# Cross-attention of layer 0: values taken with the weights as the stationary operand, denominators by an extra column, and a transpose after the division

## The chip, the cores and the metric

One core of a Trainium2 chip runs the whole program in one launch. The metric is the device time in microseconds (us); the median of three runs of the kernel before is 985.59 us (984.96 to 985.84).

## The reference

A stack of four layers works on x of 8 batches x 256 tokens x 128 features, in float32. Each layer is a cross-attention to a context of 8 x 64 tokens and then a feed-forward part; every part adds its output to x. The change touches only the first part, the attention of layer 0:

```
q  = layernorm(x) @ Wq                 # 16 heads of 8 features
k, v = context @ Wkv                   # one head of 8 features, shared by all 16
sim = (q * 8**-0.5) . k                # 16 heads x 64 keys for each token
attn = softmax(sim - max(sim))
x  = x + (attn . v, heads side by side) @ Wo
```

What has to be computed for one token and one head is a sum over 64 keys of weight times value (8 numbers) and the sum of the 64 weights, by which the 8 numbers are divided.

## The kernel before, in words

The program is written by hand for each engine: TensorE (`pe`), VectorE (`dve`), ScalarE (`act`), GpSimd (`pool`) and the DMA queue (`sp`) each have one list of instructions that runs in order, and semaphores tie them together. The tokens are 16 tiles of 128. The attention of layer 0 is a software pipeline over `for t in range(NT + 3)`, written once in each engine's block; in turn t tile t gets its similarities and older tiles their later steps. For tile u the steps are these.

- **Similarities** (`similarities`, TensorE, called S below): two products with 64 rows each, 512 columns each, into two PSUM banks. VectorE takes the maximum over the keys (L1343) and subtracts it into `simS` (L1346). ScalarE takes the exponential into `simE` (L874).
- **Weights transposed** (`weights_T`, T below): eight 128x128 transposes with `ident` (L1820) put keys on partitions. One chunk of 128 partitions holds the 64 keys of two heads. ScalarE copies the 1024 columns to `simET` (`weight_rows`, recorded at L813).
- **Values** (`values`, V below): 16 products. The stationary operand is a strip of 32 columns of `vstrip` (the values) or of `ostrip` (ones), the moving operand is a chunk of `simET` with 128 columns. Each product writes 32 partitions of bank 6. Four such products for four different groups of 32 partitions follow each other. What comes out is already transposed: features on partitions, tokens in columns, and beside it the denominators, repeated for each feature. VectorE takes the reciprocal of the 128x128 denominators (L1354) and multiplies (L1355) into `y0T`.
- **Output** (`outputs0`, O below): `y0T` times `wo0`, then VectorE adds it to X (L1359).

The order on TensorE in an ordinary turn t is S(t), T(t-1), V(t-2), O(t-3). In the turns 2, 6 and 10, called grouped, four transposes and the projection for the queries of the next four tiles stand among these (`token_rows`, `queries`), and T is cut in two halves. VectorE has, in turn t, the maximum and subtraction of tile t, the reciprocal and product of tile t-2 and the addition of tile t-3; in turn 5 also the statistics of the slot embeddings (`slot_stats`, L1309 to L1318), and after every fourth addition the statistics of the next layer norm (`ln_stats`). After turn 15 the slot transposes (L1884), the next layer norm's transposes (L1789) and the first logits of layer 0's feed-forward part (`logits_slots`) come in between the last steps, and the feed-forward part waits for the last addition to X.

All float32 products are recorded as two instruction pairs (LDWEIGHTS and MATMUL) each; transposes as one pair.

Of the kernel before, what the change touches and what calls it, by code (L numbers as in the profile page):

```python
# [5 lines left out]
ALU = mybir.AluOpType  # L6
# [40 lines left out]
def build_program(nc, A, out):  # L47
    with ExitStack() as ctx:
        def sb(name, shape, dt=F32):
            return ctx.enter_context(nc.sbuf_tensor(name, shape, dt))  # L50

        def sem(name):
            return ctx.enter_context(nc.semaphore(name))
# [50 lines left out]
        wk3 = sb("wk3", [P, D])  # L104
        wv3 = sb("wv3", [P, D])
        wo3 = sb("wo3", [P, D])


        xw = sb("xw", [P, 2 * T + 8 * P], F32R)
# [45 lines left out]
        simE = carve(2, H0 * C)  # L155
        simET = carve(2, H0 * C)
        krep = carve(B * C)
        vstrip = carve(B, 2, P // 4)
        ostrip = carve(2, P // 4)
        y0T = carve(2, P)  # L160
        mx0 = carve(2, H0)
        rden0 = carve(P)
        ctxTd = carve(B * 2 * C)
        slot_raw = carve(ES // P, D)
        slot_n = carve(ES // P, D)
# [155 lines left out]
        se_T = sem("se_T")  # L321
        kv_mm = sem("kv_mm")
        krep_done = sem("krep_done")
        vstrip_done = sem("vstrip_done")
        kbd_done = [sem("kbd_first"), sem("kbd_rest")]
        q_mm = sem("q_mm")
        q_sb = sem("q_sb")
# [4 lines left out]
        et_sb = sem("et_sb")  # L332
        av_ready = sem("av_ready")
        y_ready = sem("y_ready")
        out_ready = sem("out_ready")
        bl_ready = sem("bl_ready")
        bmax_done = sem("bmax_done")
# [237 lines left out]
        def _(pool):  # L575
# [14 lines left out]
                               pattern=[[-1, P]], channel_multiplier=1).then_inc(consts, 1)  # L590
            pool.wait_ge(consts, 1)

            then(pool.memset(headmask[:, :], 1.0))
            then(pool.affine_select(out=headmask[:, :], in_=headmask[:, :], compare_op=ALU.is_ge, fill=0.0, base=0,
                                    pattern=[[-HD, H0]], channel_multiplier=1))
            then(pool.affine_select(out=headmask[:, :], in_=headmask[:, :], compare_op=ALU.is_ge, fill=0.0, base=HD - 1,
                                    pattern=[[HD, H0]], channel_multiplier=-1))
            then(pool.tensor_tensor(rowmask[:, :], headmask[:, 0:H0 // 2], headmask[:, H0 // 2:H0], ALU.add))
            pool.memset(vstrip, 0.0)
            then(pool.memset(ostrip, 0.0))  # L600
            for par in range(2):
                for r in range(2):
                    at = 16 * par + HD * r
                    last = pool.memset(ostrip[C * r:C * r + C, par, at:at + HD], 1.0)
            last.then_inc(consts, 1)
            pool.wait_ge(consts, 2)
            pool.tensor_copy(identb[:, :], ident[:, :])

            def ln_power(L, g):
                s = slice(4 * g, 4 * g + 4)  # L610
# [200 lines left out]
        def _(act):  # L811
            def copy(dst, src):
                return act.activation(dst, src, ACT.Copy)  # L813
# [27 lines left out]
            def queries(g):  # L841
                act.wait_ge(q_mm, g + 1)
                act.activation(qT[:, 512 * g:512 * g + 512], bank(4), ACT.Copy, scale=float(HD) ** -0.5).then_inc(q_sb, 1)

            def weight_rows(u):
                act.wait_ge(et_ready, u + 1)
                if u >= 2:
                    act.wait_ge(av_ready, u - 1)
                copy(simET[:, u % 2, :], psum[:, 4:6, :].rearrange("p a n -> p (a n)")).then_inc(et_sb, 1)
# [4 lines left out]
            for t in range(NT + 3):  # L854
                g = (t + 2) // 4
                if t == 1:
                    act.wait_ge(kv_mm, 2)
                    act.wait_ge(consts, 2)
                    vps = psum[:, 6, 256:256 + B * HD].rearrange("p (b d) -> p b d", b=B)
                    for par in range(2):  # L860
                        for r in range(2):
                            at = 16 * par + HD * r
                            last = copy(vstrip[C * r:C * r + C, :, par, at:at + HD], vps[C * r:C * r + C])
                    last.then_inc(vstrip_done, 1)
                if t % 4 == 2 and t < NT - 2:
                    token_rows(g)
                    queries(g)
                if 1 <= t <= NT:
                    weight_rows(t - 1)
                if t < NT:  # L870
                    act.wait_ge(sim_used, t + 1)
                    if t >= 2:
                        act.wait_ge(et_ready, t - 1)
                    act.activation(simE[:, t % 2, :], simS[:, t % 2].rearrange("p h k -> p (h k)"), ACT.Exp).then_inc(exp_done, 1)  # L874
                if t == NT:

                    act.wait_ge(se_n, 2)
                    for g in range(2):
                        act.wait_ge(se_tp, g + 1)
                        act.activation(seT[:, 512 * g:512 * g + 512], bank(g), ACT.Identity, scale=slot_gs[:, 0:1], bias=slot_gs[:, 1:2])\  # L880
                            .then_inc(se_T, 1)
                    for g in range(2):
                        ln_evac_group(1, g)
# [329 lines left out]
        def _(dve):  # L1213
# [125 lines left out]
            for t in range(NT + 3):  # L1339
# [11 lines left out]
                if 2 <= t <= NT + 1:  # L1351
                    u = t - 2
                    dve.wait_ge(av_ready, u + 1)
                    then(dve.reciprocal(rden0, psum[:, 6, P:2 * P]))  # L1354
                    dve.tensor_tensor(y0T[:, u % 2, :], psum[:, 6, 0:P], rden0, ALU.mult).then_inc(y_ready, 1)  # L1355
                if t >= 3:
                    u = t - 3
                    dve.wait_ge(out_ready, u + 1)
# [402 lines left out]
        def _(pe):  # L1761
# [61 lines left out]
            def values(u):  # L1823
                b = u // TB
                pe.wait_ge(et_sb, u + 1)
                if u == 0:
                    pe.wait_ge(vstrip_done, 1)
                if u >= 1:
                    pe.wait_ge(y_ready, u)
                for k, w in enumerate((vstrip[:, b], ostrip)):  # L1830
                    for par in range(2):
                        for j in range(4):
                            own, at = slice(32 * j, 32 * j + 32), P * (2 * j + par)
                            last = mm(psum[own, 6, P * k:P * k + P], w[:, par, :], simET[:, u % 2, at:at + P], par == 0, par == 1)
                last.then_inc(av_ready, 1)

            def outputs0(u):
                if u == 0:
                    pe.wait_ge(w_slots, 16 * N_SLOTS)
                pe.wait_ge(y_ready, u + 1)  # L1840
                if u >= 1:
                    pe.wait_ge(x_done, u)
                mm(psum[:, 7, 0:D], y0T[:, u % 2, :], wo0[:, :]).then_inc(out_ready, 1)

            def logits_slots(k):
# [20 lines left out]
            for t in range(NT + 3):  # L1866
# [11 lines left out]
                if t == NT:  # L1878

                    pe.wait_ge(se_n, 2)  # L1880
                    pe.wait_ge(sim_used, NT - 1)
                    for g in range(2):
                        for j in range(4):
                            last = pe.transpose(psum[:, g, P * j:P * j + P], slot_n[:, 4 * g + j, :], ident[:, :])  # L1884
                        last.then_inc(se_tp, 1)
                if grouped:
                    values(t - 2)
                    queries(g)
# [12 lines left out]
                if grouped:  # L1901
                    if t >= 3:
                        outputs0(t - 3)
                    pe.wait_ge(q_sb, g + 1)
                    weights_T(t - 1, (0,)).then_inc(et_ready, 1)
                else:
                    if 2 <= t <= NT + 1:
                        values(t - 2)
                    if t >= 3:
                        outputs0(t - 3)  # L1910
# [595 lines left out]
```

## Time and profile before

| | |
|---|---|
| median of three runs | 985.59 us |
| the profiled execution's own time | 984.96 us |
| its span | 983.2 us |
| TensorE busy, whole span | 913.7 us (93%) |
| VectorE busy | 719.9 us (73%) |
| ScalarE busy | 521.5 us (53%) |
| mean granted TensorE clock | 0.967 |

The span is from the first to the last instruction in the trace; the execution's own time lies 1.8 us above it. A busy TensorE in the table is not TensorE at its peak: the ends of matmuls are modelled and contain a latency of some 0.2 us, so the time between the starts of neighbouring instructions says more than their length. "Granted clock" is 1.00 at 2.4 GHz and 0.50 at 1.2 GHz. The attention of layer 0 takes roughly the first 90 us of the span; everything behind it is the same code before and after.

### The profile page before, as it was taken

How to read it: one execution, taken by the hardware profiler on the slowest of the kernel's cores; microseconds unless marked ns; L12 is line 12 of the kernel's file. 1: busy time of each engine (PE TensorE's matmuls, PEld its weight loads, DVE VectorE, ACT ScalarE, POOL GpSimd, SP SyncE). 2: the span in 40 equal slices, each digit the busy share in tenths (PEclk: the TensorE clock that was granted, in tenths of full speed). 3: DMA queues.
4: the chain of work that ended last, by engine and by line, in shares of the span. 5: the costliest groups of instructions: out<-in, count | busy, mean ns of one | idle time of the engine just before them, and what ended most of it. 6: DMA issues, size and time to landing. Idle time of an engine off the chain costs nothing. (4 is left out here: it accounts for less than half of the span.)

```text
span 983.2 us, 16388 instructions
## 1 busy us (share of the span) xinstructions
PE 913.7 (93%) x4925; PEld 700.8 (71%) x4925; DVE 719.9 (73%) x1657; ACT 521.5 (53%) x991; POOL 572.7 (58%) x542
## 2 busy tenths in 40 slices
PE   7897998989896899999999999999999889999796
PEld 5555775666694856888888888888887766667564
DVE  6897776899464788766666666666667888886865
ACT  3455665544634256666666666666663334453354
POOL 5512544677513156777777777777776538884500
PEclk9999999999997989999999999999999689999998
DMA  6000000322000000000000000000002000000001
GB/s 193 1 2 2 1 1 11 88 71 66 12 1 27 2 9 14 25 25 24 24 24 24 24 24 24 24 24 24 25 3 108 1 0 1 1 1 1 1 11 33
DMA packets 27113, 24.01 MB, mean 24 GB/s; under 512 B 3420, under 2 KB 23988, under 8 KB 26804
## 3 DMA queue, kind: packets, MB, share of 16 engines
q1 hardware_dynamic: 27059, 23.34, 8.0%
q8 instruction: 29, 0.48, 0.2%
q14 instruction: 25, 0.20, 0.1%
HBM read 22.28 MB, written 1.05 MB: 24 GB/s over the span
## 5 line engine op out<-in xcount | busy, mean ns | idle before, releaser
L1763 PE MATMUL psum<-xw 128*128 128x512 f32 x1248 | 324.3, 396 | 3.9 <-DVE xw L1400 2.6
L664 POOL TENSOR_TENSOR hh<-arena,hh 128x512 fp32r<-128x512 f32 x176 | 228.2, 1296 | 81.7 <-ACT hh L813 80.0
L1763 PEld LDWEIGHTS psum<-xw 128*128 128x128 f32 x1248 | 233.4, 189 | 56.5 <-issue 7.2
L1599 DVE TENSOR_TENSOR psum<-psum,arena 128x512 f32<-128x512 f32 x176 | 123.1, 700 | 99.6 <-PE psum L1763 93.2
L813 ACT ACTIVATE hh<-arena 128x512 fp32r<-128x512 f32 x228 | 143.1, 629 | 47.7 <-DVE arena L1698 45.3
L1046 ACT ACTIVATE arena<-psum 128x512 f32<-128x512 f32 x176 | 105.3, 598 | 119.0 <-PE psum L1763 118.9
L1763 PE MATMUL psum<-hh,wdn 128*128 128x512 f32 x528 | 148.4, 390 | 0.2 <-POOL hh L664 0.2
L1604 DVE TENSOR_TENSOR arena<-psum,arena 128x512 f32<-128x512 f32 x176 | 121.7, 692 | 8.9 <-DVE psum L1599 2.9
L1763 PEld LDWEIGHTS psum<-hh,wdn 128*128 128x128 f32 x528 | 98.9, 188 | 21.1 <-POOL hh L664 0.5
L1763 PE MATMUL psum<-arena 128*32 128x128 f32 (+7 forms) x1032 | 94.0, 307 | 12.8 <-ACT arena L813 6.5
L612 POOL TENSOR_TENSOR rstd<-veps,neghalf 128x4 f32<-128x4 f32 x28 | 28.2, 1010 | 106.1 <-DVE veps L1238 76.0
L1763 PEld LDWEIGHTS psum<-arena 128*32 128x32 f32 (+4 forms) x1032 | 69.1, 148 | 25.0 <-issue 11.4
L813 ACT ACTIVATE arena<-psum 128x512 f32<-128x512 f32 (+7 forms) x84 | 57.1, 694 | 50.4 <-PE psum L1763 19.6
L701 POOL TENSOR_TENSOR hh<-arena,hh 128x512 fp32r<-128x512 f32 x48 | 62.1, 1295 | 33.3 <-ACT hh L813 31.8
L764 POOL TENSOR_TENSOR tail<-tail 128x512 f32<-128x512 f32 x32 | 33.3, 1041 | 43.4 <-DVE tail L1370 43.4
L1763 PE MATMUL psum<-hh,w2r 128*128 128x512 f32 x144 | 46.7, 417 | 2.0 <-POOL hh L701 1.0
L624 POOL TENSOR_TENSOR xw<-egu,xw 128x256 fp32r<-128x256 f32 x32 | 27.6, 864 | 31.8 <-ACT xw L813 31.5
L891 ACT ACTIVATE tail<-arena,tail 128x256 f32<-128x256 f32 x64 | 32.0, 500 | 26.1 <-DVE tail L1333 26.1
L928 ACT ACTIVATE tail<-psum,ebias 128x512 f32<-128x512 f32 x32 | 22.0, 688 | 44.5 <-PE psum L1763 36.9
L635 POOL TENSOR_TENSOR arena<-arena,xn (+1 forms) x32 | 42.8, 1343 | 1.2 <-ACT xn L813 1.2
L1690 DVE SCALAR_TENSOR_TENSOR arena<-psum,arena 128x512 f32<-128x512 f32 x48 | 33.1, 691 | 11.7 <-PE psum L1763 9.6
L1763 PE MATMUL psum<-xw,w2r 128*128 128x512 f32 x144 | 41.6, 401 | 0.0
(288 smaller groups left out, 1536.1 us busy)
## 6 DMA issues: line engine op xcount, KB each, us to landing
egu<-in_w SPq DMA_DIRECT2D x44, 128.0 KB, 2.0
egu<-in_egu SPq DMA_DIRECT2D x16, 256.0 KB, 2.6
edn<-in_w SPq DMA_DIRECT2D x44, 64.0 KB, 1.8
edn<-in_edn SPq DMA_DIRECT2D x16, 128.0 KB, 2.0
arena<-in_w SPq DMA_DIRECT2D x1, 1536.0 KB, 6.8
X<-in_x SPq DMA_DIRECT2D x4, 256.0 KB, 4.6
arena<-in_conv SPq DMA_DIRECT2D x1, 1024.0 KB, 8.8
out<-X SPq DMA_DIRECT2D x4, 256.0 KB, 2.3
```

The source lines that it names most:

```text
L612: pool.tensor_tensor(rstd[:, s], veps[:, s], neghalf[:, s], ALU.pow).then_inc(ln_rstd, 1)
L635: pool.tensor_tensor(part, part, wide(shift_row(b).unsqueeze(1), 2, N), ALU.subtract).then_inc(pt_shifted, 1)
L664: pool.tensor_tensor(hh[:, s % 4, 1, :], h1[:, s % 2, :], hh[:, s % 4, 0, :].bitcast(F32), ALU.subtract).then_inc(hh_lo, 1)
L701: pool.tensor_tensor(hh[:, n % 4, 1, :], h2[:, n % 2, :], hh[:, n % 4, 0, :].bitcast(F32), ALU.subtract).then_inc(hh_lo, 1)
L764: pool.tensor_tensor(qb[:, k % 4], qb[:, k % 4], wide(recB[:, k % 4].unsqueeze(2), 2, N), ALU.mult)\
L813: return act.activation(dst, src, ACT.Copy)
L891: last = act.activation(qb[:, k % 4, c, :], logit_part(k // 4, 2 * (k % 4) + c, 1).rearrange("p a n -> p (a n)"), ACT.Exp, scale=-1.0, bia ...
L1046: act.activation(sil[:, k, :], bank(k), ACT.Silu).then_inc(nl_done, 1)
L1599: dve.tensor_tensor(bank(2 + k), bank(2 + k), sil[:, k, :], ALU.mult).then_inc(prod_done, 1)
L1604: dve.tensor_tensor(h1[:, k, :], bank(2 + k), rwb[:, s // 4, own], ALU.mult).then_inc(hid_done, 1)
L1690: dve.scalar_tensor_tensor(v2w[:, n % 3, :], bank(q), 0.0, cB[:, 0 if n < 4 * NG else 1, 512 * q:512 * q + 512], ALU.max, ALU.mult)\
L1763: return pe.matmul(dst, lhsT=lhsT, rhs=rhs, start=start, stop=stop)
```

## The change

The roles of the operands in V are exchanged. The transposed weights of two heads (a 128x128 chunk of `simET`) are now stationary, eight of them, and the moving operand is `vaug`, 18 columns: for each of the two heads 8 value columns and one column of ones. What comes out has tokens on partitions and, per head, 8 sums and one denominator. VectorE's reciprocal has 16 elements per partition in place of 128, and its product of 128x128 reads the denominators broadcast over the 8 features. Since O needs features on partitions, a new step follows: TensorE transposes `y0` (`outputs_T0`, called T0 below) and ScalarE copies the result to `y0T` (`output_rows`). In turn t, T0(t-3) stands behind T(t-1) and ahead of V(t-2), in grouped turns behind `token_rows`; `output_rows(t-3)` stands behind `weight_rows(t-1)` and ahead of the exponential, in grouped turns ahead of `queries`. GpSimd's constants at the start change (`vaug` in place of `vstrip` and `ostrip`, and an array `ltmask` that nothing reads).

```diff
+        ltmask = sb("ltmask", [P, 8, 8])
...
-        vstrip = carve(B, 2, P // 4)
-        ostrip = carve(2, P // 4)
+        vaug = carve(B, 2, HD + 1)
+        y0 = carve(2, H0, HD)
         y0T = carve(2, P)
         mx0 = carve(2, H0)
-        rden0 = carve(P)
+        rden0 = carve(2, H0)
...
@@ GpSimd, constants
-            pool.memset(vstrip, 0.0)
-            then(pool.memset(ostrip, 0.0))
-            for par in range(2):
-                for r in range(2):
-                    at = 16 * par + HD * r
-                    last = pool.memset(ostrip[C * r:C * r + C, par, at:at + HD], 1.0)
-            last.then_inc(consts, 1)
-            pool.wait_ge(consts, 2)
-            pool.tensor_copy(identb[:, :], ident[:, :])
+            then(pool.affine_select(out=ltmask[:, :, :], in_=ltmask[:, :, :], compare_op=ALU.is_ge, fill=0.0, base=-1,
+                                    pattern=[[1, 8], [-1, 8]], channel_multiplier=0))
+            then(pool.memset(vaug, 0.0))
+            pool.memset(vaug[0:C, :, 0, HD:HD + 1], 1.0)
+            then(pool.memset(vaug[C:P, :, 1, HD:HD + 1], 1.0))
+            pool.tensor_copy(identb[:, :], ident[:, :]).then_inc(consts, 1)
...
@@ ScalarE
+            def output_rows(u):
+                act.wait_ge(yT_ready, u + 1)
+                if u >= 2:
+                    act.wait_ge(out_ready, u - 1)
+                copy(y0T[:, u % 2, :], psum[:, 7, 256:384]).then_inc(yT_sb, 1)
...
-                    for par in range(2):
-                        for r in range(2):
-                            at = 16 * par + HD * r
-                            last = copy(vstrip[C * r:C * r + C, :, par, at:at + HD], vps[C * r:C * r + C])
-                    last.then_inc(vstrip_done, 1)
+                    copy(vaug[0:C, :, 0, 0:HD], vps[0:C])
+                    copy(vaug[C:P, :, 1, 0:HD], vps[C:P]).then_inc(vaug_done, 1)
                 if t % 4 == 2 and t < NT - 2:
                     token_rows(g)
+                if t % 4 == 2 and t < NT - 2:
+                    if t >= 3:
+                        output_rows(t - 3)
                     queries(g)
-                if 1 <= t <= NT:
                     weight_rows(t - 1)
+                else:
+                    if 1 <= t <= NT:
+                        weight_rows(t - 1)
+                    if t >= 3:
+                        output_rows(t - 3)
...
@@ VectorE
-                    then(dve.reciprocal(rden0, psum[:, 6, P:2 * P]))
-                    dve.tensor_tensor(y0T[:, u % 2, :], psum[:, 6, 0:P], rden0, ALU.mult).then_inc(y_ready, 1)
+                    av = psum[:, 6, 0:H0 * (HD + 1)].rearrange("p (h k) -> p h k", k=HD + 1)
+                    then(dve.reciprocal(rden0[:, u % 2, :], av[:, :, HD]))
+                    if u >= 2:
+                        dve.wait_ge(yT_ready, u - 1)
+                    dve.tensor_tensor(y0[:, u % 2], av[:, :, 0:HD], wide(rden0[:, u % 2, :].unsqueeze(2), H0, HD), ALU.mult)\
+                        .then_inc(y_ready, 1)
...
@@ TensorE
-                for k, w in enumerate((vstrip[:, b], ostrip)):
-                    for par in range(2):
-                        for j in range(4):
-                            own, at = slice(32 * j, 32 * j + 32), P * (2 * j + par)
-                            last = mm(psum[own, 6, P * k:P * k + P], w[:, par, :], simET[:, u % 2, at:at + P], par == 0, par == 1)
+                for j in range(H0 // 2):
+                    w = 2 * (HD + 1)
+                    last = mm(psum[:, 6, w * j:w * j + w], simET[:, u % 2, P * j:P * j + P],
+                              vaug[:, b].rearrange("p h k -> p (h k)"))
                 last.then_inc(av_ready, 1)
+
+            def outputs_T0(u):
+                pe.wait_ge(y_ready, u + 1)
+                if u >= 1:
+                    pe.wait_ge(x_done, u)
+                pe.transpose(psum[:, 7, 256:384], y0[:, u % 2].rearrange("p h k -> p (h k)"), ident[:, :]).then_inc(yT_ready, 1)
 
             def outputs0(u):
                 if u == 0:
                     pe.wait_ge(w_slots, 16 * N_SLOTS)
-                pe.wait_ge(y_ready, u + 1)
-                if u >= 1:
-                    pe.wait_ge(x_done, u)
+                pe.wait_ge(yT_sb, u + 1)
...
+                if grouped and t >= 3:
+                    outputs_T0(t - 3)
                 if grouped:
                     values(t - 2)
                     queries(g)
...
                 else:
+                    if t >= 3:
+                        outputs_T0(t - 3)
                     if 2 <= t <= NT + 1:
                         values(t - 2)
```

## Rows read from the trace of the kernel before

**Rows 1.** Stretches: length, busy (x instructions) per engine, granted clock, DMA share, GB/s.
```profile
60.00:70.00 10.00, 8.97 (x105) 5.89 (x105) 9.65 (x21) 5.78 (x7) 3.09 (x3) 1.00 0.01 2
```

**Rows 2.** Timeline, one ordinary turn: start us, length us, engine, line, operation.
```profile
69.65 0.30 PEld L1763 LDWEIGHTS psum<-arena 64*128 64x128 f32 x4
...
70.94 0.86 PEld L1820 LDWEIGHTS psum<-ident,arena 128*128 128x128 f32 x8 [0.99 <-ACT arena L874]
...
71.10 1.22 DVE L1343 TENSOR_REDUCE arena<-psum 128x16 f32<-128x1024 f32 x1
71.97 0.81 PEld L1763 LDWEIGHTS psum<-arena 128*32 128x32 f32 x32 [0.17 <-issue]
...
72.36 1.23 DVE L1346 TENSOR_TENSOR arena<-psum,arena 128x1024 f32<-128x1024 f32 x1
72.98 0.30 PEld L1763 LDWEIGHTS psum<-wo,arena 128*128 128x128 f32 x2 [0.20 <-issue]
...
73.39 0.30 PEld L1763 LDWEIGHTS psum<-arena 64*128 64x128 f32 x4
...
73.61 1.06 ACT L874 ACTIVATE arena<-arena 128x1024 f32<-128x1024 f32 x1 [0.51 <-DVE arena L1346]
```

**Rows 3.** Timeline at the end of the stage: 128*128 work behind 128*128 work.
```profile
88.40 0.30 PEld L1763 LDWEIGHTS psum<-wo,arena 128*128 128x128 f32 x2 [0.20 <-issue]
...
88.62 0.73 PEld L1763 LDWEIGHTS psum<-xnT,seT 128*128 128x128 f32 x4
```

**Rows 4.** Projection of the values (starts: first to last us), then a whole-span group.
```profile
L1763 PE MATMUL psum<-wv,arena x16: 256/256/277, 13.4 to 15.1; 128*128 128x8 f32 x16
...
L1763 PE MATMUL psum<-arena 128*128 128x129 f32 x256 | 28.8, 275 | 0.3 <-issue 0.3
```

**Rows 5.** Groups of the whole span: reciprocals of two sizes.
```profile
L1354 DVE RECIPROCAL arena<-psum 128x128 f32<-128x128 f32 x16 | 15.2, 951 | 4.4 <-PE psum L1763 4.3
...
L1370 DVE RECIPROCAL tail<-tail 128x2 f32<-128x2 f32 x32 | 5.1, 160 | 0.4 <-ACT tail L891 0.4
```

**Rows 6.** Timeline, ScalarE's copies from PSUM, of 64 and of 512 columns.
```profile
16.14 0.89 ACT L813 ACTIVATE arena<-psum 64x64 f32<-64x64 f32 x4
...
20.46 0.60 ACT L813 ACTIVATE xnT<-psum 128x512 f32<-128x512 f32 x1 [0.45 <-PE psum L1800]
```

**Rows 7.** Timeline, similarities: the first behind the first grouped turn, and the last.
```profile
23.94 0.30 PEld L1763 LDWEIGHTS psum<-arena 64*128 64x128 f32 x4 [0.17 <-issue]
...
77.17 0.30 PEld L1763 LDWEIGHTS psum<-arena 64*128 64x128 f32 x4
```

**Rows 8.** Timeline, the grouped turn 10 and the T after it.
```profile
56.50 0.30 PEld L1763 LDWEIGHTS psum<-arena 64*128 64x128 f32 x4
...
57.56 0.42 PEld L1800 LDWEIGHTS psum<-ident,xn 128*128 128x128 f32 x4 [0.76 <-issue]
...
61.56 0.30 PEld L1763 LDWEIGHTS psum<-arena 64*128 64x128 f32 x4 [0.17 <-issue]
...
63.69 0.86 PEld L1820 LDWEIGHTS psum<-ident,arena 128*128 128x128 f32 x8 [1.83 <-ACT arena L874]
```

**Rows 9.** Timeline, slot statistics on VectorE and the V that follows.
```profile
35.87 1.64 DVE L1312 BATCH_NORM_STATS2 arena<-arena 128x6 f32<-128x128 f32 x8
...
39.85 1.08 PE L1763 MATMUL psum<-arena 128*32 128x128 f32 x32 [2.37 <-DVE arena L1355]
```

**Rows 10.** Timeline, the last tile: T and the last addition.
```profile
83.79 0.86 PEld L1820 LDWEIGHTS psum<-ident,arena 128*128 128x128 f32 x8 [2.14 <-ACT arena L874]
...
90.65 0.29 DVE L1359 TENSOR_TENSOR X<-X,psum 128x128 f32<-128x128 f32 x1
```

**Rows 11.** Stretches around two falls of the clock, columns as in rows 1.
```profile
14.00:17.30 3.30, 2.36 (x21) 2.11 (x20) 3.23 (x11) 1.82 (x5) 1.50 (x2) 1.00 1.03 338
17.30:20.70 3.40, 3.40 (x17) 1.55 (x20) 2.83 (x4) 2.32 (x3) 3.24 (x4) 0.51 0.71 202
41.20:44.60 3.40, 3.40 (x12) 2.17 (x10) 2.90 (x6) 0.60 (x1) 2.79 (x2) 0.51 0.00 0
```

More of the change, by code:

```diff
@@ L323, in build_program @@
         krep_done = sem("krep_done")
-        vstrip_done = sem("vstrip_done")
+        vaug_done = sem("vaug_done")
         kbd_done = [sem("kbd_first"), sem("kbd_rest")]
@@ L334, in build_program @@
         y_ready = sem("y_ready")
+        yT_ready = sem("yT_ready")
+        yT_sb = sem("yT_sb")
         out_ready = sem("out_ready")
@@ L591, in _ @@
             pool.wait_ge(consts, 1)
-            then(pool.memset(headmask[:, :], 1.0))
+            pool.memset(headmask[:, :], 1.0)
+            then(pool.memset(ltmask[:, :, :], 1.0))
             then(pool.affine_select(out=headmask[:, :], in_=headmask[:, :], compare_op=ALU.is_ge, fill=0.0, base=0,
@@ L1826, in values @@
                 if u == 0:
-                    pe.wait_ge(vstrip_done, 1)
+                    pe.wait_ge(vaug_done, 1)
                 if u >= 1:
                     pe.wait_ge(y_ready, u)
-                for k, w in enumerate((vstrip[:, b], ostrip)):
-                    for par in range(2):
-                        for j in range(4):
-                            own, at = slice(32 * j, 32 * j + 32), P * (2 * j + par)
-                            last = mm(psum[own, 6, P * k:P * k + P], w[:, par, :], simET[:, u % 2, at:at + P], par == 0, par == 1)
-                last.then_inc(av_ready, 1)
+                for j in range(H0 // 2):
+                    w = 2 * (HD + 1)
+                    last = mm(psum[:, 6, w * j:w * j + w], simET[:, u % 2, P * j:P * j + P],
+                              vaug[:, b].rearrange("p h k -> p (h k)"))
+                last.then_inc(av_ready, 1)
+            def outputs_T0(u):
[3 more added lines that the diff above has]
+                pe.transpose(psum[:, 7, 256:384], y0[:, u % 2].rearrange("p h k -> p (h k)"), ident[:, :]).then_inc(yT_ready, 1)
             def outputs0(u):
```

## The prediction

> **What bounds the kernel now.** I read the stretches of ten microseconds first, because the change lies in the first 90 us alone. Between 60 and 70 us VectorE is busy for 9.65 of 10 us and TensorE for 8.97 [rows 1]: VectorE is full, TensorE nearly. Then the timeline of one ordinary turn, read by starts [rows 2]. S(13) starts at 69.65 and S(14) at 73.39: 3.74 us for a turn. On VectorE the maximum starts at 71.10, the subtraction at 72.36 (1.26) and runs 1.23, and the reciprocal of 0.95 [rows 5], product and addition fill the rest of the turn. On TensorE the pieces of a turn are, from start to start: T to V 1.03 (70.94 to 71.97), V to O 1.01, O to the next S 0.41. S itself takes 1.06 where the next step needn't wait (56.50 to 57.56) [rows 8]; here T starts 1.29 after S, since it waits for the exponential (0.99 us of idle weight loader). So TensorE alone could do a turn in 1.06 + 1.03 + 1.01 + 0.41 = 3.51 us, only 0.23 below the present one. VectorE sets the turn and TensorE stands close behind: whatever is taken from the one and given to the other counts almost in full.
>
> **Gaps on TensorE.** In rows 2 the eight loads of T take 0.86 us, but V starts 1.03 after them; the 32 loads of V take 0.81, but O starts 1.01 after; O's two loads (0.11 apart) are done after 0.22, S starts after 0.41. At each of these places 0.17 to 0.20 us pass, and at each the shape of the array's tile changes (64\*128, 128\*128, 128\*32). Where one 128\*128 step follows another there is no gap although semaphores are waited on too: O starts at 88.40 and the logits behind it at 88.62, 0.22 for two loads [rows 3]. The Trainium skill has a rule for this, "TensorEngine Tiling (Array Packing)", section Key Properties: changing the tiling mode drains TensorE, changing only the tile does not. Rows 2 and 3 agree with it. I take it that gaps stand at changes of shape; the other reading, a gap at every hand-over with a wait, is a rival below.
>
> **The change, part by part.**
>
> *V on TensorE.* Before: 32 instruction pairs with 32 weight columns, 0.81 us and a gap on either side, 0.17 + 0.81 + 0.20 = 1.18. After: 8 products are 16 pairs with 128 weight columns and 18 moving ones. The nearest row is the projection of the values, 128x8 with 128\*128 weights: 16 starts in 13.4 to 15.1, 0.113 apart, at clock 1.00 [rows 11]. With 129 moving columns the group of 256 takes 28.8 us, also 0.1125 each [rows 4]. So from 8 to 129 moving columns the price is the same, it is the weights that are paid, and 18 columns lie between: 16 x 0.1125 = 1.80 us. Bounds: not under the 0.107 of T's loads (1.71), and not over the sum with both gaps (2.17).
>
> *T0 on TensorE.* One more pair, 0.11 us as in T (0.86 / 8). It stands between T and V, all 128\*128, so the gaps before and behind V go. Sum: V and T0 take 1.80 + 0.11 = 1.91 where 1.18 stood, +0.73 per turn. The ordinary turn on TensorE becomes 3.51 + 0.74 = **4.25 us**.
>
> The Trainium skill would price V lower: "TensorE: Matmul & The Clock Gate", section Back-to-back issue gap, gives about 81 ns per matmul for streams of weight load and matmul with 128 columns. By that V would be an estimated 16 x 0.081 = 1.30. Rows 4, at 0.1125, don't bear it out, and the sum goes by them.
>
> *VectorE.* The reciprocal falls from 951 ns for 128 elements to somewhere between 160 (2 elements) and 951; along the line through both rows, 6.3 ns per element, 16 elements take 0.25 us [rows 5]. The product stays 128x128. VectorE's turn becomes 3.74 - 0.70, about 3.05 us: covered by TensorE's 4.25. The gain of 0.70 is real and buys nothing beyond the 0.23 that TensorE leaves.
>
> *ScalarE.* Copying 128 columns from PSUM lies between 0.22 (0.89 / 4 for 64) and 0.60 (512) [rows 6]; by the line 0.28. It waits behind `weight_rows`, which starts when T is done and takes about 1.0: T0's result is in SBUF some 1.1 + 1.05 + 0.28 = 2.45 us after T's start, O wants it after 0.86 + 0.11 + 1.80 = 2.77. Hidden, with 0.3 us to spare; at 0.60 it is just hidden. What is queued behind it is the exponential. A tile's way from S through maximum, subtraction and exponential to its own T takes at least 1.15 for S, 1.26, 1.25 and 1.06 [rows 2] and some 0.1 between, 4.8 us; the new TensorE comes to that T 4.25 + 1.06 = 5.3 after S. Also hidden, closely.
>
> *Start-up.* GpSimd's constants and the fewer copies at turn 1 lie beside work that waits for DMA and VectorE: 0.
>
> **The sum.** From S(3) at 23.94 to S(15) at 77.17 are 53.23 us [rows 7]. After the change these twelve turns are:
> - seven ordinary ones, 4.25 each: 29.75.
> - three behind a grouped turn (3, 7, 11). There T waits for the exponential, which ScalarE does late: S at 61.56, T at 63.69, 2.13 [rows 8]. This stays. 2.13 + 0.86 + 0.11 + 1.80 + 0.41 = 5.31 each: 15.93.
> - grouped turn 10: 61.56 - 56.50 = 5.06 [rows 8], plus 0.74: 5.80.
> - grouped turn 6, where VectorE is late by the slot statistics. Before, V(4) stood until 39.85, 2.37 us idle, [rows 9] and the clock then fell [rows 11]. The statistics start at 35.87; with reciprocal 0.95, product and addition ahead of V's release at 39.85 they last some 2.56. Counted from S(5): subtraction at 2.44, statistics from 3.6 to 6.15, short reciprocal, product and addition until 6.95, T0(3) at 6.97, V, then 2.40 until S(7) as in turn 10: 11.28. S(6) is at 4.25, so turn 6 takes 7.03.
>
> Together 58.5: **+5.3**. Ahead of S(3): V(0) is on the path, partly at the low clock: +0.7. Behind S(15): T(15) stood 6.62 us after it, because VectorE was late with its maximum; TensorE stood idle for 2.14 [rows 10]. VectorE now has time in every turn: I put the end of the statistics after addition 11 at 1.6 us after S(15), and 1.26 + 1.25 + 1.06 + 0.05 later T comes, at 5.2: -1.4. From T(15) to the last addition were 6.86 us (90.65 - 83.79) [rows 10]. After: T 0.86, T0 0.11, V(14) 1.80, O 0.22, norm transposes 0.86, T0 0.11, V(15) 1.80, O 0.22, logits 0.86, then T0(15), copy, O and addition 0.9: 7.75, +0.9. Sum of all: 0.7 + 5.3 - 1.4 + 0.9 = +5.5.
>
> *The clock.* At 17.3 it falls to 0.51 (1.2 GHz) for 3.4 us, after a stretch at 1.00 with the narrow 128x8 products, an idle time and a T; it falls again at 41.2 [rows 11], after the idle time before V(4) [rows 9]. The new V is work of just that narrow kind. In ordinary turns S and T stand close on either side of it and I expect full clock; in the three turns with the 1 us wait for T, and in turn 6, a fall is possible. One costs at most half its 3.4 us, 1.7. The fall at 41.2 is already out of turn 6's new figure. I add **1.0** for one of these at less than its bound.
>
> 984.96 (the execution's own time, span 983.2 plus 1.8) + 6.5 = 991.5. The median lies 0.6 above this execution: **992 us**.
>
> **Rivals.**
> 1. *Gaps at every hand-over.* If what costs 0.17 to 0.20 is the wait and not the shape, T to T0, T0 to V and V to O keep one each: 0.54 per turn over 14 turns, +7.5: 999.5. For it: each of the gaps in rows 2 has waits as well. Against it: rows 3.
> 2. *The clock stays low often.* If the narrow V brings it down in four or five turns, +1.5 each on top: 998 to 1000. For it: rows 11. Against it: T and S in the same turn.
> 3. *The weights load as fast as before's, or nearly.* The strips of V before are loaded 0.81 / 32 = 0.025 apart for 32 columns [rows 2], T's 128 columns 0.107; if the new V lay halfway, at 0.066 a pair, it would take 1.06. TensorE's ordinary turn would be 3.51, and VectorE's 3.05 under it; fifteen turns give back 0.74 each, 11 us, and the relief of VectorE in turn 6 and at T(15) is left over: 991.5 - 11 = 980.5, **faster than before. It decides from 0.085 us per pair down** (15 x 16 x 0.027 = 6.5, the whole forecast loss). For it: the moving columns are few, so nothing but the load is left to pay. Against it: two groups in rows 4 at 0.1125 with 8 and with 129 columns. By the Trainium skill's 81 ns of above (TensorE: Matmul & The Clock Gate, Back-to-back issue gap) the time would be an estimated 991.5 - 7.5 = 984, on the edge of this rival.
> 4. *TensorE's surplus is absorbed.* Turn 6 and the end lose more stall than I counted (idle 2.37 and 2.14 us before), and no clock falls: 986 to 988.
>
> **How the numbers follow.** Forecast 0.62 (988 to 995), rival 1 0.10, rival 2 0.09, rival 3 0.08, rival 4 0.11. The range 986 to 998 leaves out most of rival 3 and the top of 1 and 2. A measurement of this kernel tells about 0.2%, 2 us, from no change. Slower than 987.6: forecast, rivals 1 and 2 and a little of 4: 0.83. Within: most of rival 4, part of 3: 0.11. Faster: the rest of 3: 0.06.
>
> **What the changed profile would show.** V: 16 pairs 128\*128 with 128x18, starts 0.11 apart, T0 one pair, no gap between T, T0, V and O, one of 0.2 before S. Ordinary turns 4.25 us from S to S, TensorE with no idle time in them, VectorE at about seven tenths in 60 to 70 us. Reciprocal near 0.25 us. The last addition of the stage near 96 us. Everything behind it as before but for shifted falls of the clock. I am wrong if the pairs of V lie clearly under 0.1 us apart, if O waits for ScalarE, or if the turns in which the granted clock is 0.50 are many.

## The result, and the profile after

The changed kernel takes 993.88 us in the median (991.86 to 996.98), the kernel before beside it 985.72: ratio 1.0078, 95% interval 1.0048 to 1.0107. By these medians, of four executions each, it is slower by 8.2 us; 992 was forecast, 986 to 998 was the range. All 25 executions of the changed kernel on record for this result lie between 990.05 and 999.47 us, with a median of 992.99. The profiled execution is the longest of them, 999.47 us with a span of 997.7; another execution of the same kernel, taken later, took 990.75 us with a span of 989.0. The two are read side by side. The last addition of this stage starts at 103.27 us in the one and at 95.72 in the other, so 7.55 of the 8.7 us between the spans lie in this stage, and there the granted clock is what differs; 1.15 lie behind it, in code that is the same.

First the ordinary turn, in the timeline of the changed kernel (start, length, engine, line, operation; L1836 is T, L1856 is T0, the 128x128 loads at L1779 are V, and the 64x128 loads S). It answers to [rows 2] (times in us; LDWEIGHTS is the load of a stationary operand):

```profile
55.29 0.30 PEld L1779 LDWEIGHTS psum<-arena 64*128 64x128 f32 x4
...
55.82 0.60 PE L1779 MATMUL psum<-arena 64*128 64x512 f32 x2
56.35 0.85 PEld L1836 LDWEIGHTS psum<-ident,arena 128*128 128x128 f32 x8 [0.76 <-ACT arena L886]
...
57.17 0.14 PEld L1856 LDWEIGHTS psum<-ident,arena 128*128 128x128 f32 x1
...
57.28 1.87 PEld L1779 LDWEIGHTS psum<-arena 128*128 128x128 f32 x16
...
57.48 1.19 ACT L815 ACTIVATE arena<-psum 128x1024 f32<-128x1024 f32 x2 [1.64 <-PE psum L1836]
...
58.98 1.06 ACT L886 ACTIVATE arena<-arena 128x1024 f32<-128x1024 f32 x1 [0.31 <-DVE arena L1358]
59.07 0.30 PEld L1779 LDWEIGHTS psum<-wo,arena 128*128 128x128 f32 x2
...
59.28 0.26 DVE L1367 RECIPROCAL arena<-psum 128x16 f32<-128x16 f32 x1 [0.34 <-PE psum L1779]
59.49 0.30 PEld L1779 LDWEIGHTS psum<-arena 64*128 64x128 f32 x4
```

T to V takes 0.93 (56.35 to 57.28) with T0 in it, V to O 1.79, O to S 0.42: V's 16 loads stand 0.112 apart, and there is no gap between T, T0, V and O, only the one ahead of S. VectorE's reciprocal is down from 951 ns to about 0.25 us and now waits for TensorE; ScalarE's copy of 128 columns lies inside the 1.19 at 57.48 (two copies merged) and ends 0.4 us before O. TensorE holds the turn: 4.20 us from S (55.29) to S (59.49).

Now the clock. The stretches of the profiled execution, then of the later one (columns as in [rows 1]):

```profile
20.00:40.00 20.00, 17.83 (x125) 13.21 (x124) 15.35 (x47) 10.20 (x14) 8.94 (x10) 1.00 0.01 1
40.00:60.00 20.00, 18.84 (x124) 14.70 (x126) 14.10 (x30) 9.43 (x13) 7.86 (x6) 0.91 0.00 1
60.00:80.00 20.00, 18.97 (x101) 14.27 (x99) 11.17 (x25) 7.64 (x12) 3.09 (x3) 0.75 0.01 1
80.00:95.00 15.00, 14.70 (x101) 11.69 (x97) 10.79 (x24) 6.51 (x9) 3.09 (x3) 0.88 0.01 2
...
69.80:83.50 13.70, 13.70 (x54) 10.24 (x54) 6.45 (x10) 3.43 (x5) 0.00 (x0) 0.50 0.00 0
```

```profile
20.00:40.00 20.00, 18.03 (x125) 13.40 (x125) 14.71 (x45) 10.17 (x14) 8.75 (x10) 1.00 0.00 1
40.00:60.00 20.00, 18.56 (x131) 14.24 (x132) 14.76 (x32) 9.47 (x13) 8.06 (x6) 1.00 0.00 1
60.00:80.00 20.00, 18.97 (x138) 14.62 (x136) 14.71 (x30) 9.98 (x15) 3.09 (x3) 1.00 0.01 2
80.00:95.00 15.00, 14.35 (x117) 12.81 (x115) 8.32 (x26) 8.76 (x14) 3.09 (x3) 1.00 0.00 1
```

Look at the granted clock, the third figure from the end of a line. The later execution has 1.00 throughout. The profiled one has a whole 13.7 us at 0.50, 1.2 GHz, from 69.8 on. What TensorE did just before was this (profiled execution): a grouped turn, S(11), one microsecond without work until the exponential was there, T, T0 and the narrow V, in the middle of which the clock fell. The later execution has the same wait and the same V in turn 11 and no fall, so these do not bring one about each time.

```profile
65.24 0.30 PEld L1779 LDWEIGHTS psum<-arena 64*128 64x128 f32 x4 [0.17 <-issue]
...
67.37 1.09 PE L1836 MATMUL psum<-ident,arena 128*128 128x128 f32 x8 [1.00 <-ACT arena L886]
...
68.30 2.10 PEld L1779 LDWEIGHTS psum<-arena 128*128 128x128 f32 x16
...
71.05 0.51 PEld L1779 LDWEIGHTS psum<-arena 64*128 64x128 f32 x4 [0.23 <-issue]
...
74.82 3.54 PEld L1779 LDWEIGHTS psum<-arena 128*128 128x128 f32 x16
...
79.01 0.51 PEld L1779 LDWEIGHTS psum<-arena 64*128 64x128 f32 x4 [0.23 <-issue]
```

At the low clock V takes 3.54 and the turn 7.96 (71.05 to 79.01) in place of 4.20. Turns 11, 12 and 13 together cost 6.4 us more than their like elsewhere. The 0.91 between 40 and 60 us is a shorter fall, 3.4 us from 42.6 on, in turn 6, behind the wait ahead of T0(3).

### The profile page after: what moved, and what is told of

Read it like the earlier page. It is cut to its first block and busy times, and to the rows that moved or that the text cites. A ratio compares the mean times of both kernels' runs of the same rounds, so it can differ in the third digit from the quotient of the medians.

```text
span 997.7 us, 15949 instructions
## 1 busy us (share of the span) xinstructions
PE 930.0 (93%) x4685; PEld 722.5 (72%) x4685; DVE 709.9 (71%) x1657; ACT 522.4 (52%) x1005; POOL 572.8 (57%) x541
## 5 line engine op out<-in xcount | busy, mean ns | idle before, releaser
L1779 PE MATMUL psum<-xw 128*128 128x512 f32 x1248 | 322.7, 394 | 3.9 <-DVE xw L1416 2.6
L1779 PEld LDWEIGHTS psum<-xw 128*128 128x128 f32 x1248 | 232.3, 188 | 56.0 <-issue 7.2
L1779 PE MATMUL psum<-hh,wdn 128*128 128x512 f32 x528 | 148.4, 390 | 0.2 <-POOL hh L666 0.2
L1779 PE MATMUL psum<-arena 128*128 128x18 f32 (+7 forms) x776 | 111.5, 322 | 10.3 <-ACT arena L815 6.5
L1779 PEld LDWEIGHTS psum<-hh,wdn 128*128 128x128 f32 x528 | 98.9, 188 | 21.1 <-POOL hh L666 0.5
L1779 PEld LDWEIGHTS psum<-arena 128*128 128x128 f32 (+3 forms) x776 | 90.1, 196 | 19.9 <-ACT arena L815 9.3
L815 ACT ACTIVATE arena<-psum 128x512 f32<-128x512 f32 (+8 forms) x98 | 59.7, 634 | 64.6 <-PE psum L1836 31.2
L1779 PE MATMUL psum<-hh,w2r 128*128 128x512 f32 x144 | 46.7, 416 | 2.2 <-POOL hh L703 0.8
L1779 PE MATMUL psum<-xw,w2r 128*128 128x512 f32 x144 | 41.7, 402 | 0.0
```

The source lines that it names most:

```text
L1779: return pe.matmul(dst, lhsT=lhsT, rhs=rhs, start=start, stop=stop)
```

## The experiments

**Half the loads.** V with 4 products of 36 columns:

```diff
-                for j in range(H0 // 2):
-                    w = 2 * (HD + 1)
-                    last = mm(psum[:, 6, w * j:w * j + w], simET[:, u % 2, P * j:P * j + P],
-                              vaug[:, b].rearrange("p h k -> p (h k)"))
+                for j in range(H0 // 4):
+                    w = 4 * (HD + 1)
+                    pair = b // 2 * 2
+                    last = mm(psum[:, 6, w * j:w * j + w], simET[:, u % 2, P * j:P * j + P],
+                              vaug[:, pair:pair + 2].rearrange("p b h k -> p (b h k)"))
```

> The changed kernel, but V has 4 products of 36 moving columns in place of 8 of 18: the same columns go through, half the weights are loaded (the chunks of heads 8 to 15 are left out, so these heads' sums are not computed). Theory (V costs what its 16 weight loads cost, 0.112 us each): V takes 0.90 in place of 1.79, TensorE alone could do a turn in 3.3, the way from S through the exponential (4.8 us) then holds the turn at about 3.55; thirteen turns give back 0.65, some 8 to 9 us, and falls of the clock become rare: about 981 to 983, faster than the kernel before. Rival (V's price is a fixed latency or the moving columns): V stays near 1.8 and the time near 990 to 994.

Measured: 985.05 us (981.67 to 986.53), ratio to before 0.9987 (0.9975 to 0.9999). One ordinary turn of it:

```profile
65.28 0.30 PEld L1779 LDWEIGHTS psum<-arena 64*128 64x128 f32 x4
...
66.34 0.86 PEld L1836 LDWEIGHTS psum<-ident,arena 128*128 128x128 f32 x8 [0.76 <-ACT arena L886]
...
67.27 0.97 PEld L1779 LDWEIGHTS psum<-arena 128*128 128x128 f32 x8
...
68.71 0.30 PEld L1779 LDWEIGHTS psum<-wo,arena 128*128 128x128 f32 x2 [0.47 <-ACT arena L815]
...
69.13 0.30 PEld L1779 LDWEIGHTS psum<-arena 64*128 64x128 f32 x4
```

Half the loads with the same moving columns in all are 0.97 where 1.87 stood: V pays per pair, whether 18 or 36 columns move. This kernel halves the number of pairs together with the weight columns, so it doesn't separate the two; that the columns count is read from V before, whose pairs with 32 weight columns start 0.025 apart [rows 2]. But the turn is 3.85, not 3.55, and O now waits 0.47 for ScalarE: the copy to `y0T` stands behind 1024 columns of weights. The step that was "hidden, with 0.3 us to spare" binds as soon as V shrinks. The time expected, 981 to 983, was missed by 2 to 4 us; 0.3 us in each of twelve turns is of that size.

**One pair per product (fp32r).** `simET` is laid into `hh` and `vaug` into `wdn`, both fp32r tensors idle in this stage:

```diff
-        simET = carve(2, H0 * C)
+        simET = hh[:, 0:2].rearrange("p a b n -> p a (b n)")
...
-        vaug = carve(B, 2, HD + 1)
+        vaug = wdn[:, 0].rearrange("p h n -> p (h n)")[:, 0:B * 2 * (HD + 1)].rearrange("p (b h k) -> p b h k", b=B, h=2)
...
```

GpSimd's constants for `vaug` are written through a float32 view of it; that is all else that differs.

> The changed kernel with simET and vaug in the rounded 32-bit type (fp32r), so that each of V's 8 products is one pair in place of two. Theory (a pair costs its weight load, 0.11): V takes 0.90 in place of 1.79, as in the run with half the loads, but with all heads computed; turn about 3.55, time 981 to 983. Rival (an fp32r load of 128 columns costs more than half of the two float32 loads): V between 0.9 and 1.8, time between 983 and 991.

Measured: 985.07 us (981.53 to 987.07), ratio 0.9987 (0.9972 to 1.0003). V is 8 pairs in 0.97 us, so an fp32r load costs what a float32 load costs and there are half as many; the turn is 3.85 with the same wait of 0.47 for ScalarE. The time, expected at 981 to 983, was missed for the same reason.

**VectorE's gain alone.** In the kernel before:

```diff
-                    then(dve.reciprocal(rden0, psum[:, 6, P:2 * P]))
-                    dve.tensor_tensor(y0T[:, u % 2, :], psum[:, 6, 0:P], rden0, ALU.mult).then_inc(y_ready, 1)
+                    then(dve.reciprocal(rden0[:, 0:H0], psum[:, 6, P:P + H0]))
+                    dve.tensor_tensor(y0T[:, u % 2, :].rearrange("p (h k) -> p h k", k=HD), psum[:, 6, 0:P].rearrange("p (h k) -> p h k", k=HD),
+                                      wide(rden0[:, 0:H0].unsqueeze(2), H0, HD), ALU.mult).then_inc(y_ready, 1)
```

> The kernel before, but VectorE's reciprocal reads 16 columns in place of 128 and the product reads them broadcast (the division is then by the wrong denominators; V and O are as before). This is the change's gain on VectorE alone. Theory (TensorE stands 0.23 us behind VectorE, and the way through the exponential at 3.6): ordinary turns of 3.74 and 3.78 fall to 3.5 to 3.6, each of twelve gives 0.1 to 0.2, turn 6 and the wait for T(15) shrink by 0.7 to 1.4 each: 3 to 4 us, 982 to 983. Rival (VectorE's 0.70 counts in full): 0.7 in each of 15 turns, 975.

Measured: 982.48 us (980.45 to 982.97), ratio 0.9961 (0.9950 to 0.9973), in the size that was expected: 3.6 us, not the 10 that 0.70 in each turn would be. But it does not come from where it was expected. S starts in its trace at

```profile
64.20 0.30 PEld L1764 LDWEIGHTS psum<-arena 64*128 64x128 f32 x4
...
67.71 0.30 PEld L1764 LDWEIGHTS psum<-arena 64*128 64x128 f32 x4
...
71.45 0.30 PEld L1764 LDWEIGHTS psum<-arena 64*128 64x128 f32 x4
```

3.51 and 3.74 apart, where the kernel before had 3.51 and 3.74 in the same places: these turns are not VectorE's. Of the twelve turns from S(3) on only one ordinary turn (3.78 to 3.52) and turn 6 (8.89 to 6.52) shrank, and the wait for T(15). The 0.1 to 0.2 expected in each turn did not come, and turn 6 gave 2.4 in place of 0.7 to 1.4; in this trace it has no fall of the clock, in that of the kernel before it has one [rows 11]. That the sum came out as expected is luck.

**Without the new step.** T0 and the copy left out, O reads `y0`:

```diff
-                pe.wait_ge(yT_sb, u + 1)
-                mm(psum[:, 7, 0:D], y0T[:, u % 2, :], wo0[:, :]).then_inc(out_ready, 1)
+                pe.wait_ge(y_ready, u + 1)
+                if u >= 1:
+                    pe.wait_ge(x_done, u)
+                mm(psum[:, 7, 0:D], y0[:, u % 2].rearrange("p h k -> p (h k)"), wo0[:, :]).then_inc(out_ready, 1)
...
```

> The changed kernel without T0 and without ScalarE's copy: O takes y0 as it is (which leaves the transposition out of the result; all else is done). Theory (in the changed kernel TensorE holds the turn and the copy is hidden behind V): T0 costs its one weight load, turns fall from 4.20 to 4.10, 5.27 to 5.17, 5.75 to 5.65. Rival (O in fact waits for the copy now and then): more than 0.2 per turn.

Measured, in one execution: turns of 4.09 (53.83 to 57.92), 5.16 and 5.64, so T0 costs 0.11 a turn and the copy nothing; 989.28 us, with one fall of the clock, in turn 6.

```profile
53.83 0.30 PEld L1775 LDWEIGHTS psum<-arena 64*128 64x128 f32 x4
...
57.92 0.30 PEld L1775 LDWEIGHTS psum<-arena 64*128 64x128 f32 x4
```

**Gap by shape or by wait.** A product is added at the head of V, behind its waits, with 32 weight columns in one kernel (first line) and with 128 in the other (second line):

```diff
+                mm(psum[0:32, 6, 160:168], ident[:, 0:32], ident[:, 0:8])
...
+                mm(psum[:, 6, 160:168], ident[:, :], ident[:, 0:8])
```

> The changed kernel with one tiny product added between T0 and V: 32 weight columns, 8 moving ones (128*32), into unused columns of V's bank. Two loads of 32 columns are 0.05 us. Theory (gaps stand where the tile's shape changes): its turns grow by 0.05 and two gaps of 0.17 to 0.20, from 4.20 to 4.6. Rival (gaps stand where there are waits): it adds no wait, turns grow by 0.05 to 4.25.

> As the run before, but the added product is full (128*128, 8 moving columns): two loads of 128 columns, 0.22 us of work. Theory of the shape: no gap, turns from 4.20 to 4.42, so the larger product costs less than the smaller. Rival of the waits: the same 4.42, but then the smaller one at 4.25.

Measured, in one execution each: ordinary turns of 4.56 with the small product, 4.42 with the large one. The product with a quarter of the weights costs 0.36, the full one 0.22. (The times, 998.40 and 993.83 us, hold falls of the clock at different places, the small one's 10.2 us long from 17.6 on, and are not compared.) First the small, then the large one in their timelines; the first view ends ahead of V's last two loads:

```profile
73.02 0.14 PEld L1857 LDWEIGHTS psum<-ident,arena 128*128 128x128 f32 x1
...
73.33 0.14 PEld L1779 LDWEIGHTS psum<-ident 128*32 128x32 f32 x2 [0.17 <-issue]
...
73.48 1.64 PEld L1779 LDWEIGHTS psum<-arena 128*128 128x128 f32 x14
```

```profile
70.97 0.14 PEld L1857 LDWEIGHTS psum<-ident,arena 128*128 128x128 f32 x1
...
71.08 0.30 PEld L1779 LDWEIGHTS psum<-ident 128*128 128x128 f32 x2
...
71.31 1.87 PEld L1779 LDWEIGHTS psum<-arena 128*128 128x128 f32 x16
```

T0 to the small product is 0.31 for a single load, to the large one 0.11. The gap belongs to the change of shape, as [rows 3] had it: both products stand behind the same waits, and only the small one has gaps. The Trainium skill's rule (TensorEngine Tiling (Array Packing), Key Properties), that changing the tiling mode drains TensorE, agrees with it.

**The clock.** Products of `ident` fill TensorE's waits, ahead of T in turns 3, 7 and 11 and ahead of T0(3) in turn 6:

```diff
+            def fill(k, n):
+                for _ in range(n):
+                    mm(psum[:, k, 384:512], ident[:, :], ident[:, :])
...
+                if t == 6:
+                    fill(5, 5)
...
+                    if t in (3, 7, 11):
+                        pe.wait_ge(et_sb, u)
+                        fill(4, 4)
                     pe.wait_ge(exp_done, u + 1)
```

> The changed kernel, with products of ident by ident put where TensorE waits: four ahead of T in turns 3, 7 and 11 (0.86 us of work in a wait of 1.0) and five ahead of T0(3) in turn 6. Nothing is left out. Theory (the runs of the changed kernel differ by 990 to 999.5 because the clock falls in this stage in some): granted clock 1.00 from 20 to 95 us, turn 6 about 7.1, all turns at 4.20, 5.27, 5.75; time 989 to 991 with runs within 1 us of each other. Rival (the spread comes from later stages, or the narrow V itself brings the clock down): spread stays several us, median 992 to 995; or, if the fillers come too late for the wait, each adds up to 0.9 us.

Measured: 990.46 us (989.64 to 992.68), ratio to before 1.0056 (1.0037 to 1.0075). All turns are as if undisturbed: 4.20, 5.27, 5.75 and 7.12 for turn 6. The five executions lie within 3.0 us, not within the 1 expected. Then the changed kernel again, and each kind of filler alone:

> The changed kernel itself, on the same chip and beside the same runs of before as the next two. Theory (its runs differ by where the clock falls in this stage): median 992 to 995 with runs over 6 us apart, while the kernel before stays within 3. Rival (the spread was that of the other chip): within 3 us as before.

> The changed kernel with only the five products of ident ahead of T0(3) in turn 6; nothing in turns 3, 7 and 11. Theory (turn 6 holds the fall at 42 us, 1.4 us, and the three waits of 1 us for T each hold a rarer, costlier one): turn 6 at 7.1, one of the other falls still in some runs: median 991 to 993, spread 3 to 6 us. Rival (turn 6 alone is the cause): as with all fillers, 990.5 and no fall between 20 and 95 us.

> The changed kernel with only the four products ahead of T in turns 3, 7 and 11. Theory: turn 6 stays at 8.4 with its fall, the long stretch at 1.2 GHz from turn 11 on is gone, as are the slowest runs: median 991 to 992.5, spread under 4 us. Rival (the narrow V brings the clock down, not the wait beside it): long stretches at 0.50 remain, median 993 to 995.

| fillers | median | lowest to highest | timed runs |
|---|---|---|---|
| none, again | 994.71 | 990.75 to 996.63 | 4 |
| turn 6 alone | 992.46 | 989.07 to 998.79 | 8 |
| turns 3, 7, 11 alone | 991.07 | 988.38 to 999.57 | 9 |
| the kernel before | 985.98 | 983.98 to 988.96 | 16 |

These four were measured side by side on one chip. The medians are where they were expected, the spreads are not: 9.7 us for turn 6 alone (3 to 6 expected) and 11.2 for turns 3, 7 and 11 (under 4), where three executions of nine still lie at 998 and above; the kernel before spreads over 5.0, not 3. The trace with the filler of turn 6 alone has two falls, one in turn 7 and a long one again from turn 11 on:

```profile
49.30:52.70 3.40, 3.40 (x11) 1.67 (x11) 1.37 (x4) 0.54 (x1) 0.00 (x0) 0.50 0.00 0
69.80:83.40 13.60, 13.60 (x52) 10.14 (x53) 5.88 (x10) 3.17 (x5) 0.21 (x1) 0.50 0.01 1
```

The trace of the other kernel is of one of its short executions. It has no fall behind 20.3 us, and its turn 6, which has no filler, takes 7.12 us, where 8.4 with a fall was expected. Where its three long executions lose their time is not seen.

All traces together say where a fall can begin. In those with the new V at its full price there are six falls between 20 and 84 us: two in the changed kernel, in turns 6 and 11; two in that with the filler of turn 6 alone, in turns 7 and 11; one without T0, in turn 6; one with the large product, in turn 3. Each begins in a turn in which TensorE waits about 1 us or more in one place (turns 3, 7 and 11 for the exponential, turn 6 for VectorE), and none in another turn. The same waits also stand in executions without a fall.

A last run asks whether both kinds of filler together close it:

> The kernel with all fillers (turns 3, 7, 11 and 6) again, with more runs, because with only one of the two kinds of filler three of nine and four of eight runs still lay at 995 to 999.6, and five runs of the full set are few. Theory (each wait left open can bring the clock down, both kinds together close them): no run above 994, median 990 to 991. Rival (the five were luck, the narrow V itself brings the clock down in some runs): one run in three at 995 or more.

Measured: 990.92 us (989.26 to 991.53), ratio to before 1.0042 (1.0029 to 1.0056). With the first, ten executions with all fillers lie between 989.3 and 992.7; of the 29 of the changed kernel itself 13 lie at or below 992.7. But the ten were not measured beside the changed kernel on one chip, so a difference of chips is not excluded. The stretches of the last run's trace:

```profile
20.00:40.00 20.00, 19.69 (x142) 15.30 (x142) 14.69 (x45) 10.26 (x14) 8.76 (x10) 1.00 0.02 4
40.00:60.00 20.00, 19.90 (x144) 15.39 (x143) 14.76 (x32) 9.48 (x13) 8.12 (x6) 1.00 0.00 1
60.00:80.00 20.00, 19.92 (x147) 15.57 (x145) 14.71 (x30) 9.96 (x14) 3.09 (x3) 1.00 0.01 1
```

What follows: 4 to 6 us of the change's price are there without any fall in this stage behind 20 us (with all fillers 990.46 and 990.92 against 986.05 and 986.57 beside them, and 989.0 against 983.2 in the spans of the two executions). Another 2 to 4 us, in the median, are falls of the clock in some executions (992.99 and 994.71 against 990.75). They begin in turns with an empty wait. That filling both kinds of wait prevents them is likely by ten executions and not shown on one chip beside the changed kernel; what decides, in a given execution, whether the clock falls is open.

**A version that beats both.** The fp32r kernel, with T0 ahead of T, ScalarE's copy ahead of the weights, and the filler in turn 6:

```diff
-                    if 1 <= t <= NT:
-                        weight_rows(t - 1)
                     if t >= 3:
                         output_rows(t - 3)
+                    if 1 <= t <= NT:
+                        weight_rows(t - 1)
...
+                if not grouped and t >= 3:
+                    outputs_T0(t - 3)
                 if 1 <= t <= NT:
                     u = t - 1
                     pe.wait_ge(exp_done, u + 1)
...
-                    if t >= 3:
-                        outputs_T0(t - 3)
...
```

> The kernel with V in one pair per product (fp32r), and T0(t-3) ahead of T(t-1) in ordinary turns, ScalarE's copy ahead of weight_rows; five products of ident fill TensorE's wait in turn 6. Nothing is left out. Theory (at 3.85 per turn O waited for ScalarE, which copied y0T only behind 1024 columns of weights): O no longer waits, TensorE alone needs 3.4, the way through the exponential holds the turn at 3.5 to 3.6, twelve turns give 0.3 each against the run with fp32r, the clock stays up in turn 6: 979 to 981, faster than the kernel before by 5 to 6 us. Rival (3.85 is held by something else, the exponential say): turns stay at 3.85, 983 to 985.

Measured: 981.41 us (978.72 to 986.59), ratio to before 0.9955 (0.9943 to 0.9968): 4.6 us faster, a little less than the 5 to 6 expected. Ordinary turns are 3.31 and 3.63, and O follows V without a wait, so it was the copy's place that held 3.85. `simET` and `vaug` are rounded here (fp32r), and the kernel before with its own V in fp32r was not run: how much of the 4.6 us belongs to the type and how much to the new form of V is not shown. One turn:

```profile
67.25 0.97 PEld L1779 LDWEIGHTS psum<-wdn,hh 128*128 128x128 f32 x8
...
68.14 0.30 PEld L1779 LDWEIGHTS psum<-wo,arena 128*128 128x128 f32 x2
...
68.56 0.30 PEld L1779 LDWEIGHTS psum<-arena 64*128 64x128 f32 x4
...
69.99 0.28 ACT L815 ACTIVATE arena<-psum 128x128 f32<-128x128 f32 x1 [0.31 <-PE psum L1860]
```

## Why the prediction was right, point by point

- *V costs its weight loads, 16 x 0.1125 = 1.80.* Measured 1.79, and halved with half the pairs.
- *No gap between T, T0, V and O.* As measured; an added change of shape costs 0.3. Rival 1, which hung on the gaps being those of waits, falls.
- *Turns.* Forecast 4.25, 5.31, 5.80, and 7.03 for turn 6; in the undisturbed execution 4.20, 5.27, 5.75 and 7.13. From S(3) to S(15) 58.5 was forecast and 58.10 measured, against 53.23 before [rows 7]. (The term for the ordinary turn slipped in passing: its parts sum to +0.73, +0.74 was added; measured +0.69 over TensorE's own 3.51.)
- *The ends.* From S(0) to S(3) it grew by 0.63 (0.7 forecast). T(15) came 5.63 after S(15), not 5.2, since VectorE's statistics end 2.10 after S(15), not 1.6. The last addition came 8.10 after T(15), not 7.75, since T0(15), copy, O and addition take 1.25, not 0.9. Behind S(15) the forecast gained 0.5 in sum, and 0.25 was lost.

```profile
81.99 0.30 PEld L1779 LDWEIGHTS psum<-arena 64*128 64x128 f32 x4
...
87.62 0.86 PEld L1836 LDWEIGHTS psum<-ident,arena 128*128 128x128 f32 x8 [0.72 <-ACT arena L886]
...
95.72 0.29 DVE L1375 TENSOR_TENSOR X<-X,psum 128x128 f32<-128x128 f32 x1 [0.19 <-PE psum L1779]
```

- *The sum.* The span grew by 989.0 - 983.2 = 5.8 against 5.5, and part of this agreement is luck. The last addition is only 5.07 later (95.72 against 90.65), because S(0) itself stands 0.68 earlier (10.80 against 11.48), which the start-up term put at 0. The other 0.7 lie behind the stage, in code that is the same. S(0) stands at 11.48 and 11.91 in the two traces with the old start-up and at 10.59 to 11.44 in the twelve with the new one; that the change shortens the start-up is possible and not shown. The part behind the last addition takes 891.0 to 894.4 us in the traces of the changed kernel and of those that differ from it by T0 or added products only, so 1 us of a sum for a whole execution means little.
- *VectorE's gain buys nothing in ordinary turns.* With the new V it waits for TensorE; in the kernel before it alone is worth 3.6 us. What it gives here it gives in turn 6 and ahead of T(15), as the forecast had it. The sentence "VectorE sets the turn" was a wrong reading, without weight for the sum: turns of 3.51 and 3.74 stayed what they were without its 0.70. They are held by a tile's way from S through maximum, subtraction and exponential to its T, 4.80 us (S(12) at 66.14, in the line below, to T(12) at 70.94 [rows 2]), together with TensorE's own 3.51: behind a turn of 3.51 T comes 4.80 - 3.51 = 1.29 after S in place of 1.06, and the next turn takes 3.74.

```profile
66.14 0.30 PEld L1763 LDWEIGHTS psum<-arena 64*128 64x128 f32 x4
```

- *The clock, +1.0.* This term was sized wrongly. I bounded a fall by 3.4 us at half speed, as long as those in [rows 11], 1.7 us each. In turn 6 it cost 8.45 - 7.13 = 1.3, as thought; from turn 11 on it lasted 13.7 us and cost 6.4. The places were right: turns 3, 7, 11 and 6. The median execution of this kernel lies 2 to 4 us above the undisturbed one. So the forecast of 992 lies 1 to 3 us under the medians (992.99 of 25 executions, 993.88 and 994.71 of four each). Rival 2 had the size of the longest executions; its mechanism, that the narrow V brings the clock down, is not shown, since the same V runs at 1.00 throughout in the execution of 990.75.
- *Rival 3* would have been too hopeful: V took 0.112 a pair, not 0.066, and even a V of 0.97 gives 985, not 980.5, since ScalarE's copy then holds the turn at 3.85.

## What to carry to other kernels

In this case a product with few moving columns costs its weight loads and nothing less, so exchanging the roles of two operands to save the vector engine is priced in weight columns: 512 before (four groups of 32 side by side) against 1024 after, per pass (0.81 against 1.79 us for both passes). When the engine that is to take the work stands within 0.23 us of holding the turn itself, nearly its whole increase counts: the turns of 3.51 and 3.74 both became 4.20. A step that is hidden should be written down with its margin, for it is the next bound when the cover shrinks.

## What the runs showed of the hardware that I had not expected

- A float32 product with 32 weight columns and 8 moving ones costs more (0.36 us) than one with 128 weight columns (0.22) when it stands among full-width work, because of two changes of shape. Each is shown in one execution, in all its ordinary turns.
- The clock, once down in this stage, stayed at 1.2 GHz for 13.7 us although TensorE had work all the time by the profile (busy 13.70 of 13.70 in the stretch above); in the kernel before the falls of this stage last 3.4 us [rows 11]. Two of the traces have such a stretch, both from turn 11 on.
- Filler products in waits of 1 us cost no time: all turns stay at 4.20, 5.27, 5.75 and 7.12. Ten executions with both kinds lie between 989.3 and 992.7 us, 29 of the changed kernel between 990.1 and 999.5, but not measured beside them on one chip; with either kind alone some reach 998.8 and 999.6.
- fp32r weights load at the price of float32 weights, 0.11 us for 128 columns (8 loads in 0.97, the last one's own 0.19 in it); what is saved is the second pass.
